# Attention values weighed one unit later, exchange loads put ahead of the write, x moved and split in five pieces

## What is computed

```
q = x @ Wq.T                                        # 20 heads of 32 channels
k, v = text @ Wk.T, text @ Wv.T                     # 77 keys
k_ip, v_ip = ip @ Wk_ip.T, ip @ Wv_ip.T             # 77 keys
out = softmax(q k^T / sqrt(32)) v + softmax(q k_ip^T / sqrt(32)) v_ip
y = out @ Wo.T + bo + x
```

## Time and profile before

| | |
|---|---|
| median of three runs | 569.11 us (567.46 to 569.16) |
| profiled execution, time | 568.92 us |
| profiled execution, span of the core | 567.0 us |
| outside the span | 1.9 us |
| busy: PE, DVE, ACT, POOL | 506.1, 415.3, 368.3, 298.2 us |
| DMA, mean over the span | 263 GB/s, 149.16 MB in all |

### The profile page before, as it was taken

How to read it: one execution, slowest core, us unless ns; L and a number is a source line. 1 busy time by engine, 2 the same in 40 slices (tenths; PEclk the granted TensorE clock), 3 DMA queues, 4 the chain that set the end, 5 groups by cost and what they waited for, 6 DMA issues and landing times.

```text
span 567.0 us, 15760 instructions
## 1 busy us (share of the span) xinstructions
PE 506.1 (89%) x5314; PEld 427.5 (75%) x5314; DVE 415.3 (73%) x654; ACT 368.3 (65%) x1634; POOL 298.2 (53%) x259
## 2 busy tenths in 40 slices
PE   7999667789898999899979999898989899899786
PEld 7999555677786888787868878687878787778574
DVE  0025589987887799979896989698869789788812
ACT  0135558686776687868785878677767768677610
POOL 2033335565555567575665575656556665754610
PEclk9999669999997999999998999899989899999989
DMA  8991256969988998999888989888988898888891
GB/s 298 412 369 77 76 184 214 279 236 283 280 272 269 274 299 272 294 288 298 280 263 288 288 268 279 279 269 288 295 261 291 259 297 272 251 253 266 269 275 57
DMA packets 96366, 149.16 MB, mean 263 GB/s; under 512 B 10832, under 2 KB 81232, under 8 KB 96080
## 3 DMA queue, kind: packets, MB, share of 16 engines
q1 hardware_dynamic: 96336, 148.76, 82.3%
HBM read 85.81 MB, written 62.91 MB: 262 GB/s over the span
## 4 chain that ended last, share of the span: by engine, by line
DMA 53%; PE 21%; SPq 16%; DVE 4%; issue 4%; ACT 2%; DVEq 0%
DMA bounce_d<-turned 49%; SPq L293 14%; PE q_ps L611 5%; PE x_ps L611 3%; PE s_ps L737 3%; DMA p_last<-bounce_d 3%; PE pv_ps L648 2%; PE pv_ps L737 2%; PE s_ps L636 2%; DVE wo_lo L503 1%; PE v_ps L737 1%; DMA stage<-wk_in 1%; DVE row_neg L511 1%; DVE turned L531 1%; PE s_ps L687 1%
## 5 line engine op out<-in xcount | busy, mean ns | idle before, releaser
L350 POOL TENSOR_TENSOR probs<-probs,row_inv 128x616 f32<-128x616 f32 x160 | 194.5, 1236 | 188.3 <-DVE row_inv L543 188.3
L391 ACT ACTIVATE probs<-s_ps,row_neg 128x77 f32<-128x77 f32 x640 | 197.7, 322 | 81.3 <-DVE row_neg L511 81.2
L511 DVE TENSOR_REDUCE row_neg<-s_ps 128x8 f32<-128x616 f32 x160 | 120.5, 794 | 75.9 <-PE s_ps L636 75.9
L391 ACT ACTIVATION_READ_ACCUMULATOR probs<-s_ps,row_neg 128x1 f32 x640 | 130.0, 203 | 0.0
L531 DVE STREAM_TRANSPOSE turned<-probs 128x512 f32<-128x512 f32 (+1 forms) x160 | 125.0, 819 | 1.5 <-POOL probs L350 1.5
L611 PEld LDWEIGHTS q_ps<-x_hi,wq_hi 128*128 128x128 f32 x400 | 61.1, 198 | 33.1 <-issue 33.1
L611 PE MATMUL q_ps<-x_hi,wq_hi 128*128 128x256 f32 x400 | 85.1, 312 | 0.0
L648 PE MATMUL pv_ps<-p_main,v 128*32 128x256 f32 x640 | 52.9, 403 | 32.1 <-DMA p_last<-bounce_d 31.9
L636 PE MATMUL s_ps<-keys,q 32*128 32x154 f32 x1280 | 65.7, 319 | 12.6 <-issue 6.8
L611 PE MATMUL q_ps<-x_hi,wq_lo 128*128 128x256 f32 x400 | 75.8, 288 | 0.0
L611 PE MATMUL q_ps<-x_lo,wq_hi 128*128 128x256 f32 x400 | 75.1, 286 | 0.0
(11 more groups left out here) (69 smaller groups left out, 603.5 us busy)
## 6 DMA issues: line engine op xcount, KB each, us to landing
bounce_d<-turned SPq DMA_DIRECT2D x80, 640.0 KB, 4.0
p_main<-bounce_d SPq DMA_DIRECT2D x320, 128.0 KB
x_raw<-x_in SPq DMA_DIRECT2D x16, 640.0 KB, 6.6
res<-x_in SPq DMA_DIRECT2D x75, 128.0 KB, 3.2
y_out<-res SPq DMA_DIRECT2D x75, 128.0 KB, 2.9
p_last<-bounce_d SPq DMA_DIRECT2D x80, 104.0 KB
stage<-wk_in SPq DMA_DIRECT2D x6, 640.0 KB, 8.6
stage<-wv_in SPq DMA_DIRECT2D x6, 640.0 KB, 9.4
```

What stands on the lines that cost most here:

```text
L350: nc.gpsimd.tensor_tensor(rows[:, :, keys], rows[:, :, keys], row_inv[:, u.slot, :, br].unsqueeze(2) .broadcast_to([P, GROUP * SUB, size]) ...
L391: done = nc.scalar.activation(rows[:, cols], s_ps[:, j, cols], ACT.Exp, bias=row_neg[:, j, i:i + 1], accum_out=row_sum[:, j, i:i + 1])
L511: nc.vector.tensor_reduce(row_neg[:, heads_of(half)], by_row(s_ps[:, heads_of(half), 0:SUB * BLK]), AXIS.X, ALU.max, negate=True).then_inc ...
```

## The change

Four edits that belong together.

1. VALUE_LAG is 5: `weigh_values`, `attn_high` and `attn_low` of a unit stand one unit later. The last tile's code gets one more of each.
2. SP issues all five loads of unit u-3 first, then the write of u-1 (before: three loads of u-2, the write, two loads).
3. x is loaded in five DMAs of 128 KB, one in each unit; ACT and POOL split it piece by piece (`X_HIGH`, `X_LOW` say in which unit). The first two tiles are still moved and split whole.
4. ACT takes `attn_high` between `exp` and the second `exp_direct`; DVE takes `attn_low` before `invert`.

```diff
-VALUE_LAG = 4
+VALUE_LAG = 5
+X_HIGH = [[(1, 3)], [(1, 4)], [], [(2, 0), (2, 1)], [(2, 2)]]
+X_LOW = [[(1, 2)], [(1, 3)], [(1, 4)], [], [(2, 0), (2, 1)]]
...
             def emit(u):
                 ahead, old, new = u.tile_plus(2), u.plus(-OUT_LAG - 1), u.plus(GROUPS - OUT_LAG - 2)
-                if u.plus(-2).exists():
-                    load_turned(u.plus(-2), range(0, 3))
+                if u.plus(-3).exists():
+                    load_turned(u.plus(-3))
                 if u.plus(-1).exists():
                     bounce(u.plus(-1))
-                if u.plus(-2).exists():
-                    load_turned(u.plus(-2), range(3, KEY_BLOCKS))
...
-                if u.g == 2 and ahead.exists():
-                    wait(sp, x_lo_done, u.tile(1, 2))
-                    sp.dma_start(x_raw[:], x_d[ahead.t, ahead.batch]).then_inc(x_loaded, DMA)
+                if ahead.exists():
+                    wait(sp, x_lo_done, u.tile(GROUPS, GROUPS + u.g + 1))
+                    sp.dma_start(x_raw[:, u.g, :], x_d[ahead.t, ahead.batch, :, u.g, :]).then_inc(x_loaded[u.g], DMA)
...
+            def split_x_chunk(u, k):
+                wait(pool, x_hi_done, u.tile(GROUPS, k + 1))
+                nc.gpsimd.tensor_tensor(x_lo[:, u.batch, k], x_raw[:, k], x_hi[:, u.batch, k].bitcast(F32),
                                         ALU.subtract).then_inc(x_lo_done, 1)
...
             def exps(u):
                 exp_direct(u, range(0, 1))
                 exp(u)
+                if u.plus(-VALUE_LAG).exists():
+                    attn_high(u.plus(-VALUE_LAG))
                 exp_direct(u, range(1, PAIR))
...
+            def split_x_chunk(u, k):
+
+                wait(act, x_loaded[k], u.tile(DMA, -DMA))
+                if k == 0:
+                    wait(act, q_acc, u.number(1, -GROUPS))
+                nc.scalar.activation(x_hi[:, u.batch, k], x_raw[:, k], ACT.Copy).then_inc(x_hi_done, 1)
...
                 exps(u)
-                if u.plus(-VALUE_LAG).exists():
-                    attn_high(u.plus(-VALUE_LAG))
                 if nxt.exists():
                     keep_q(nxt)
                 if chunk.exists():
                     add_bias(chunk)
...
-                invert(u)
                 if u.plus(-VALUE_LAG).exists():
                     attn_low(u.plus(-VALUE_LAG))
+                invert(u)
...
+                weigh_values(final.plus(-4))
                 project_out(LAST.plus(-4))
```

More of the change, by code:

```diff
@@ L162, in build @@
         v_ps = psum("v_ps")
-        x_loaded = sem("x_loaded")
+        x_first = sem("x_first")
+        x_loaded = [sem(f"x_loaded{k}") for k in range(GROUPS)]
         wq_loaded, wo_loaded = sem("wq_loaded"), sem("wo_loaded")
@@ L256, in _ @@
             pieces(wv_d, 0, wv_loaded, range(3, 4))
-            sp.dma_start(x_raw[:], x_d[0, 0]).then_inc(x_loaded, DMA)
+            sp.dma_start(x_raw[:], x_d[0, 0]).then_inc(x_first, DMA)
             pieces(wv_d, 0, wv_loaded, range(4, len(PIECES)))
@@ L261, in _ @@
             pieces(wv_d, 1, wv_loaded)
-            sp.wait_ge(x_lo_done, 1)
-            sp.dma_start(x_raw[:], x_d[0, 1]).then_inc(x_loaded, DMA)
+            sp.wait_ge(x_lo_done, GROUPS)
+            sp.dma_start(x_raw[:], x_d[0, 1]).then_inc(x_first, DMA)
             sp.dma_start(wo_raw[:], wo_d).then_inc(wo_loaded, DMA)
@@ L281, in bounce, with load_turned @@
                              turned[:, u.slot].rearrange("p b q k -> p (b q k)")).then_inc(bounced[u.slot], DMA)
-            def load_turned(u, blocks):
+            def load_turned(u):
                 uses = u.uses_of_slot(DMA)
[L286 to L291, removed]
+                if u.fixed and u.number() == 0:
+                    sp.wait_ge(padded, 3)
+                wait(sp, pv_ready[u.slot], uses)
+                wait(sp, bounced[u.slot], uses)
+                for b in range(KEY_BLOCKS):
                     to = p_main[rows_of(b), u.slot] if b < BLOCKS else p_last[0:REST, u.slot]
@@ L315, in _ @@
             final = LAST.plus(GROUPS - 1)
+            load_turned(final.plus(-2))
             bounce(final)
             for u in (final.plus(-1), final):
-                load_turned(u, range(KEY_BLOCKS))
+                load_turned(u)
             load_residual(LAST.plus(-1))
@@ L338, in split_x @@
             def split_x(u):
-                wait(pool, x_hi_done, u.tile(1, 1))
+                wait(pool, x_hi_done, u.tile(GROUPS, GROUPS))
                 nc.gpsimd.tensor_tensor(x_lo[:, u.batch], x_raw[:], x_hi[:, u.batch].bitcast(F32),
+                                        ALU.subtract).then_inc(x_lo_done, GROUPS)
+            def split_x_chunk(u, k):
+                wait(pool, x_hi_done, u.tile(GROUPS, k + 1))
+                nc.gpsimd.tensor_tensor(x_lo[:, u.batch, k], x_raw[:, k], x_hi[:, u.batch, k].bitcast(F32),
                                         ALU.subtract).then_inc(x_lo_done, 1)
@@ L358, in emit @@
             def emit(u):
-                ahead, last, chunk = u.tile_plus(1), u.plus(-1), u.plus(-OUT_LAG - 1)
+                last, chunk = u.plus(-1), u.plus(-OUT_LAG - 1)
                 if last.exists():
@@ L363, in emit @@
                     add_residual(chunk)
-                if u.g == 1 and ahead.exists() and not (u.fixed and u.number() == 1):
-                    split_x(ahead)
+                for later, k in X_LOW[u.g]:
+                    tile = u.tile_plus(later)
+                    if tile.exists() and not (tile.fixed and tile.number() < 2 * GROUPS):
+                        split_x_chunk(tile, k)
             split_x(Unit(0, 0))
@@ L404, in exps @@
                 exp(u)
+                if u.plus(-VALUE_LAG).exists():
+                    attn_high(u.plus(-VALUE_LAG))
                 exp_direct(u, range(1, PAIR))
             def split_x(u):
-                wait(act, x_loaded, u.tile(DMA, DMA))
-                wait(act, q_acc, u.number(1, -GROUPS))
-                nc.scalar.activation(x_hi[:, u.batch], x_raw[:], ACT.Copy).then_inc(x_hi_done, 1)
+                wait(act, x_first, u.tile(DMA, DMA))
+                nc.scalar.activation(x_hi[:, u.batch], x_raw[:], ACT.Copy).then_inc(x_hi_done, GROUPS)
+            def split_x_chunk(u, k):
[3 more added lines that the diff above has]
+                nc.scalar.activation(x_hi[:, u.batch, k], x_raw[:, k], ACT.Copy).then_inc(x_hi_done, 1)
             def add_bias(c):
@@ L425, in emit @@
             def emit(u):
-                ahead, nxt = u.tile_plus(2), u.plus(Q_AHEAD)
+                nxt = u.plus(Q_AHEAD)
                 chunk = u.plus(-OUT_LAG)
                 exps(u)
-                if u.plus(-VALUE_LAG).exists():
-                    attn_high(u.plus(-VALUE_LAG))
                 if nxt.exists():
@@ L434, in emit @@
                     add_bias(chunk)
-                if u.g == GROUPS - 1 and ahead.exists():
-                    split_x(ahead)
+                for later, k in X_HIGH[u.g]:
+                    tile = u.tile_plus(later)
+                    if tile.exists() and not (tile.fixed and tile.number() < 2 * GROUPS):
+                        split_x_chunk(tile, k)
             def weight_high(hi, raw, loaded, done):
@@ L487, in _ @@
             final = LAST.plus(GROUPS - 1)
+            attn_high(final.plus(-4))
             add_bias(LAST.plus(-4))
@@ L593, in _ @@
                 turn(final, part)
-            for m in (-3, -2):
+            for m in (-4, -3, -2):
                 attn_low(final.plus(m))
@@ L620, in project_q @@
                     if u.g == 0:
-                        wait(pe, x_lo_done, u.tile(1, 1))
+                        wait(pe, x_lo_done, u.tile(GROUPS, GROUPS))
                     wait(pe, q_done, u.number())
```

## The result

| | median of the runs | profiled: time, span |
|---|---|---|
| before | 568.3 us | 568.92, 567.0 |
| changed | 536.2 us (534.4 to 541.4) | 537.34, 535.5 |

The ratio is 0.945, with a 95% interval of 0.938 to 0.953. Forecast were 536.0 us in a range of 527 to 553.

The account below looks back on a forecast made before the run. SP's round through the write's landing bounds the kernel, by PE's waits and slow clock. Span 567.0 - 420.58 + 70 x 5.55 (388.5) + 1.1 - 1.9 = 534.1 us, plus 1.9 outside: 536.0 us, range 527 to 553.

Parts of the forecast that it names:

- What bounds before: On SP: write, wait for its landing, issue three loads, next write; 5.57 us a round, 8.1 in one of five.
- PE's waits and the slow clock go: On PE before `weigh_values`: waits for the last load, about 29 us, vanish, and the half-speed clock after them too.
- the split of the excess into 29 and 10 us: Of 39.8 us too much over 70 units, PE's waits for the last load explain about 29, the slow clock the rest.
- The new bound, 5.55 us from 5.28 + 0.27: Round scores, maxima, exponentials, scores: 5.28 us, plus 0.27 for `attn_high` inside it, above PE's 5.44.
- Part 1, "the write loses nothing": On SP: five loads ahead of the write end at T + 4.6 us after scores start, when `turned` is ready.
- Part 2, x in pieces at no cost: Five x pieces on DMA, POOL and ACT cost nothing; a POOL piece takes 0.62 us within 2.4 us idle.
- Part 3, the move as a draw: `attn_high` between the exponentials on ACT costs 0.11 us a unit and saves 0.14 through earlier attention for `project_out`.
- Start and end: Units 5 to 8 get 0.27 us each, +1.1 us; the end after the last scores changes by -1.9 us.
- The signs: Chain led by ACT, DVE and scores; PE's load waits near zero; scores 5.55 us apart; clock 1.00 in the middle.
- The sum: 567.0 - 420.58 + 388.5 + 1.1 - 1.9 = 534.1 us of span; with 1.9 outside, 536.0 us.
- PE's bound of 527 us: Rival: attention is hidden and PE's own work bounds at 5.44 us a unit, 527 us; chance 0.08.
- SP's round: Rival: SP's issuing or the DMA engines bound, unit 5.8 us giving 553.5 us, or 5.65 giving 543; chance 0.24.

## Why the prediction was right, step by step

- **What bounds before** (SP's round write, landing, three loads): right. The lag alone left it in place, lag and order together removed it. That it takes both is argued: the order alone was not run.
- **PE's waits and the slow clock go:** right. The waits fell from 31.9 us to 1.4, the clock of the stretch rose from 0.98 to 1.00; the split of the excess into 29 and 10 us was not measured by itself. About 3.4 us at half clock (worked out from a mean of 0.76 over the unit) remained in unit 9 in the first profile (6.97 us for that unit, +1.4 us), and were not there in the second.
- **The new bound, 5.55 us from 5.28 + 0.27:** right to the hundredth. The extra instruction on ACT and the move into the gap show that it is a cause and not an agreement of numbers. The estimate of 0.31 us that I had worked out from the Trainium skill (ScalarE: Activation LUTs, section What ACT_TABLE_LOAD costs) is too much for this place: the round grew by 0.27, so the measurement decides for the spacing of the rows.
- **Part 1, "the write loses nothing":** wrong in the step, right in its price. SP's issuing was sized at 5.3 to 5.4 us from rows in which p_last took 0.9 us to issue; behind the four other loads it takes 0.41 (205.34 in the changed kernel), and the five loads 2.3 us in place of 2.8. In the version with the residual load last the write stood 4.7 us after the scores, where I had 4.6. But in the change as made I named the residual load only as queued behind the slot and not as a wait of its own, for a store issued 4.9 us before. That wait cost 46.8 us on SP and put the write at up to 8.6 us after the scores. PE saw two late units of it, 1.1 us together. The landing of a store was 2.9 us in the median before, 4.8 and 4.1 in the two profiles after: I had no term for longer landings, and why they are longer was not tested.
- **Part 2, x in pieces at no cost:** right, POOL's piece took 0.75 us and not 0.62, in idle time. It should have been asked what it gains: beside the new order, nothing. The warning that I drew from the Trainium skill (DMA: Bandwidth & Descriptors, section Bandwidth) against small transfers found nothing to bite on either: the version with whole tiles was no faster. Its figures are for transfers issued from GpSimd; these are issued from SyncE.
- **Part 3, the move as a draw:** its price of 0.11 us a unit was right, its gain too small. Late attention costs 0.86 us once in five units, 0.17 in each, where I had 0.14; the mean unit with x whole is 5.58 us with the move and 5.63 without, and the move is worth about 4 us.
- **Start and end:** the start to unit 9 took 109.6 us where the sum had 110.8; the end 34.3 where it had 34.8.
- **The signs:** spacing, the place of `attn_high`, PE's waits and the clock came as forecast. The chain did not: I expected ACT, DVE and the scores to lead it, and it names POOL and issuing, with ACT at 2%. The idle time before the scores, 0.2 us on PE's weight load, is put down to issue and not to ACT, too. The extra instructions had to decide what the chain could not.
- **The sum:** the 70 units took 391.6 against 388.5, and the start and the end gave 1.7 back: 535.5 of span against 534.1. That the median fell within 0.3 us of the forecast is partly luck; the executions themselves differ by 7 us.
- Of the rivals, PE's bound of 527 us is what the version with attention in the gap reaches. SP's round was close: SP waited for a store 53 times, and that reached PE twice.

What stays open: why SP fell behind in one profile of the changed kernel and not in the other, and how much of that makes the spread of its runs; also whether the new order would do without the lag.

## What to carry to other kernels

Where a wait ends by a landing, look for the whole round: a deeper buffer alone brings nothing while the mean round is too long, and issuing the dependent loads one unit later ahead of the next write takes the landing out of it. Then list every wait that the issuing engine has, since the next round through a landing may be a small transfer's. An instruction that must go into the tightest round belongs where its engine already waits there: the same `attn_high` cost 0.27 us a unit behind `exp` and nothing ahead of it.

## What the runs showed of the hardware

- Share of the DMA engines over 1 is not saturation: the changed kernel had 1.01 at 297 GB/s over 391 us, and the version with the gap and the residual load last moved the same bytes in units shorter by 2%, at 1.03 and 305 GB/s.
- Landings became longer while the bytes moved faster: that of the write went from 4.0 to 5.8 us in the median, that of a 128 KB store from 2.9 to 4.8, in one profile, and to 4.4 and 4.1 in the other. The rate alone does not explain it, since the same program gave both; what does is open.
- The issue of the same 104 KB load on SP took 0.94 us (median) behind a write of 640 KB and one load, and 0.41 us behind four loads. What holds it there was not tested.
